# Attention and expert-layer kernel: layer norm of the first attention's scores by centred context and mean square, head rebuilt, routing of the second half of the tokens moved into the shared unit

## What is computed

```python
x = x + attention1(layernorm(x), ctx)      # kv = ctx @ W.T + b ; out = p @ kv ; sim = out @ kv.T / 16
                                           # softmax(layernorm(sim) * gamma + beta)
x = x + experts(layernorm(x))              # 8 experts, top 2, capacity 160 each for first and second choice, plus a shared one
x = x + attention2(ctx, ctx, layernorm(x)) # softmax(q.k * layernorm(x), masked)
x = x + lut_ffn(layernorm(x))              # silu(gate) * up, down; weights looked up in a table of 16
```

## Time and profile before

| | us |
|---|---|
| median of 3 runs | 328.35 |
| lowest, highest | 326.55, 332.02 |
| the profiled execution, its own time | 328.0 |
| its span in the trace | 326.3 |
| mean granted clock of PE, share of full speed | 0.965 |

### The profile page before, as it was taken

How to read it: one execution, slowest core, us unless ns; L and a number is a source line. 1 busy time by engine, 2 the same in 40 slices (tenths; PEclk the granted TensorE clock), 3 DMA queues, 4 the chain that set the end, 5 groups by cost and what they waited for, 6 DMA issues and landing times.

```text
span 326.3 us, 6015 instructions
## 1 busy us (share of the span) xinstructions
PE 305.4 (94%) x1944; PEld 262.5 (80%) x1944; DVE 239.2 (73%) x650; ACT 151.3 (46%) x358; POOL 111.6 (34%) x153
## 2 busy tenths in 40 slices
PE   8998567997999999999999999999999989979995
PEld 4654355776989899898989999899888879879994
DVE  3658987413499989898998989898986749866632
ACT  2466437533346455564546555565633532541210
POOL 7473644770000605032150604123062226234331
PEclk9998769999899999999999999999999999979998
DMA  7994018335167664939375574828033000010101
GB/s 230 371 265 105 7 42 268 123 113 148 48 178 249 142 220 97 308 63 294 94 212 167 129 252 72 294 52 229 3 40 131 1 0 2 0 35 0 34 1 64
DMA packets 26259, 41.48 MB, mean 127 GB/s; under 512 B 3898, under 2 KB 16955, under 8 KB 26236
## 3 DMA queue, kind: packets, MB, share of 16 engines
q1 hardware_dynamic: 22012, 36.46, 35.2%
q0 software_dynamic: 4224, 4.75, 8.2%
HBM read 31.37 MB, written 9.82 MB: 126 GB/s over the span
## 4 chain that ended last, share of the span: by engine, by line
PE 78%; DVE 9%; POOL 4%; issue 3%; ACT 3%; DMA 1%; SPq 0%; POOLq 0%
PE hb L715 25%; PE yb L734 24%; PE hb L849 10%; PE yb L748 5%; PE tb L648 3%; PE rb L864 3%; PE yb L553 2%; POOL xbuf_dram L498 2%; PE yb L864 1%; DVE x L1249 1%; DVE bst L1104 1%; DVE xn L1110 1%; DVE xT_lo L1262 1%; POOL rstd L461 1%; DMA xbuf_dram<-xn,put_i 1%
## 5 line engine op out<-in xcount | busy, mean ns | idle before, releaser
L734 PE MATMUL yb<-raw,h 128*128 128x256 f32 x384 | 96.7, 382 | 0.0
L1015 ACT ACTIVATE h<-hb,b 128x320 f32<-128x320 f32 (+1 forms) x80 | 44.6, 559 | 70.1 <-PE hb L715 68.7
L734 PEld LDWEIGHTS yb<-raw,h 128*128 128x128 f32 x384 | 70.3, 192 | 7.5 <-ACT h L1015 0.4
L715 PE MATMUL hb<-xT_hi,w_hi 128*128 128x320 f32 (+1 forms) x180 | 72.6, 403 | 1.4 <-DVE xT_lo L1262 1.4
L518 POOL DMA_INDIRECT xacc_dram<-ysb,slot_i x16 | 25.5, 1594 | 126.1 <-ACT ysb L883 123.6
L715 PE MATMUL hb<-xT_lo,w_hi 128*128 128x320 f32 (+1 forms) x180 | 59.3, 329 | 0.0
L715 PE MATMUL hb<-xT_hi,w_lo 128*128 128x320 f32 (+1 forms) x180 | 59.2, 329 | 0.0
L1454 DVE TENSOR_TENSOR w_lo<-raw,w_hi 128x256 fp32r<-128x256 f32 x81 | 33.6, 415 | 22.3 <-ACT w_hi L883 22.2
L1136 DVE COPY_PREDICATED pick<-bits,pick 128x536 int32<-128x536 uint8 x56 | 42.7, 762 | 0.6
L715 PEld LDWEIGHTS hb<-xT_hi,w_hi 128*128 128x128 f32 x180 | 34.4, 191 | 6.6 <-issue 2.0
L715 PEld LDWEIGHTS hb<-xT_hi,w_lo 128*128 128x128 f32 x180 | 34.6, 192 | 2.5
(11 more groups left out here) (205 smaller groups left out, 523.4 us busy)
## 6 DMA issues: line engine op xcount, KB each, us to landing
raw<-w1pack_dram SPq DMA_DIRECT2D x30, 384.0 KB, 3.5
raw<-w2pack_dram SPq DMA_DIRECT2D x30, 384.0 KB, 5.5
xbuf_dram<-h SPq DMA_DIRECT2D x8, 323.8 KB, 10.0
idx<-idx_dram SPq DMA_DIRECT2D x8, 268.0 KB, 6.1
xg<-xbuf_dram SPq DMA_DIRECT2D x8, 259.0 KB, 5.9
x<-x_dram SPq DMA_DIRECT2D x4, 256.0 KB, 4.4
xacc_dram<-x SPq DMA_DIRECT2D x2, 512.0 KB, 7.0
x<-xacc_dram SPq DMA_DIRECT2D x4, 256.0 KB, 4.6
```

The source lines that it names most:

```text
L715: mm = pe.matmul(hb[s % RING][:, 0:n], w[:, s, k * P:(k + 1) * P], a[:, turn, k, 0:n], start=(i == 0), stop=(i == len(terms) - 1))
L734: mm = pe.matmul(yb[c // 2][:, (c % 2) * D:(c % 2 + 1) * D], h, w, start=(s == 0 and c % 2 == 0), stop=(s == STEPS - 1), skip_group_check= ...
L1015: act.activation(hidden(s - 1, shared, turn), bank[:, 0:n], ACT.Gelu, bias=b1[:, expert, s - 1:s])\
```

## The change

1. **Centred context.** DVE sums each batch of `ctxT` over its 256 columns and forms `ctxc` = 256*ctx - sum (`centre`). `kvT` is projected from it without the bias row (`project`), so the scores come out with mean zero, times 256. 
2. **Mean square.** ACT squares the scores out of PSUM with a sum along the row (`squares`); POOL makes 1/sqrt from the sums (`inv_sim`). `sim_stats`, `offsets`, `standard_sim` and `gain` are gone. DVE multiplies the scores in PSUM by 1/std and gamma into SBUF in one instruction per tile, in front of the old row maximum.
3. **Head.** POOL's constants are reordered, with the first two `inv_std` among them. `values` works on half the context at a time. Idle matmuls: 12 in place of 22 ahead of `token_rows(0)`, and their wait for `gate_ok` is now for an instruction that DVE does behind `norm_x` of batches 0 and 1. The last batch's `sim_rows` comes behind `norm_x(2, 1)`; `exps(0, 3)` behind `rows_hi(1)`.
4. **Routing.** On DVE `up_rows(0)` and `low_rows(0)`, which need unit 0's step 0, come ahead of `add_probs(0, 3)`, the normalising of half 1 and `choose(0)`. On PE `token_rows(1)` goes from behind `first(0)` to behind `first(3)`, `count(0)` from there to behind `second(0)`; `logits_of(1)`, `logits_rows(1)`, `count(1)` follow in steps 3 to 5; scores 2 and 3 go from steps 4 and 5 to 6 and 7. ACT does `rows_hi(2)`, `logits_exp(0)` and `logits_copy(1)` behind the Gelu of step 3, `logits_exp(1)` behind that of step 5.

```diff
@@ gpsimd
-            for b in range(B):
-                inv_std(1, b, S * 1e-6)
-                split_lo(b, b)
-                gain(b)
+            inv_sim(0)
+            split_lo(0, 0)
+            inv_sim(1)
+            split_lo(1, 1)
+            inv_sim(2)
+            split_lo(2, 2)
             inv_std(2, 0, 1e-5)
+            inv_sim(3)
+            split_lo(3, 3)
@@ tensor
             pe.wait_ge(gate_ok, 2)
-            pe.wait_ge(proj_sb, 2 + B)
+            pe.wait_ge(consts_ok, CONSTS)
+            pe.wait_ge(kv_sb, 2)
             pe.wait_ge(exp_ok, 4)
-            keep_busy(16, rb)
+            keep_busy(8, rb)
             pe.wait_ge(xn_ok, 2)
-            keep_busy(6, rb)
+            keep_busy(4, rb)
             token_rows(0)
...
                     first(g, u, s, shared, turn)
+                    if u_is(u, 0):
+                        if s == 3:
+                            token_rows(1)
+                        elif s == 4:
+                            logits_rows(1)
+                        elif s == 5:
+                            count(1)
...
                         second(u, 0, shared, turn, loads)
+                        if u_is(u, 0):
+                            count(0)
@@ scalar
+            def squares(b):
+                act.wait_ge(sim_mm, b + 1)
                 for i in range(2):
                     tile = 2 * b + i
-                    act.activation(exp_rows(0, b)[:, i, :], hb[b % RING][:, i * S:(i + 1) * S], ACT.Identity,
-                                   bias=nmr[:, tile:tile + 1], scale=rstd[:, 1, tile:tile + 1]).then_inc(sm_in, 1)
+                    act.activation(exp_rows(0, b)[:, i, :], hb[b % RING][:, i * S:(i + 1) * S], ACT.Square,
+                                   accum_out=ssq[:, tile:tile + 1]).then_inc(ssq_ok, 1)
...
+            exps(0, 0)
+            squares(2)
+            outT_copy(3)
+            split_hi(0, 0, 0)
+            squares(3)
+            exps(0, 1)
...
-                        if s == 1:
+                        if s == 3:
+                            rows_hi(2, 1, UTOK)
+                            logits_exp(0)
                             logits_copy(1)
-                        elif s == 2:
+                        elif s == 5:
                             logits_exp(1)
@@ vector
+            def centre(b):
+                cols = slice(b * S, (b + 1) * S)
+                if b == 0:
+                    dve.wait_ge(ctx_in, 32)
+                own(dve.tensor_reduce(ctx_sum[:, b:b + 1], ctxT[0:H, cols], AX.X, ALU.add))
+                dve.tensor_scalar(ctxc[:, cols], ctxT[0:H, cols], float(S), ctx_sum[:, b:b + 1], ALU.mult, ALU.subtract)\
+                    .then_inc(ctxc_ok, 1)
...
+                    dve.scalar_tensor_tensor(out=exp_rows(0, b)[:, i, :], in0=hb[b % RING][:, i * S:(i + 1) * S],
+                                             scalar=rstd[:, 1, tile:tile + 1], in1=gamma[:, :],
+                                             op0=ALU.mult, op1=ALU.mult).then_inc(sm_in, 1)
...
             norm_x(2, 0, xn_ok)
+            norm_x(2, 1, xn_ok)
+            dve.wait_ge(gate_ok, 1)
+            dve.tensor_tensor(gate_parts[:, :, E:2 * E], gate_w[:, :, :], gate_parts[:, :, 0:E].bitcast(F32),
+                              ALU.subtract).then_inc(gate_ok, 1)
             sim_rows(3)
...
-            choose(0)
-            route(0)
-            rows_lo(2, 1, UTOK)
...
+            add_probs(0, 2, 2)
             up_rows(0, 0)
+            low_rows(0, UTOK)
+            add_probs(0, 3, 2)
+            norm_x(2, 2, xn_ok)
+            norm_x(2, 3, xn_ok)
+            choose(0)
+            rows_lo(2, 1, UTOK)
+            route(0)
             unit(0, 0, shared=True, extra=unit0_extra)
```

More of the change, by code:

```diff
@@ L468, in split_lo @@
                     .then_inc(w_lo_ok, 1)
[L470 to L483 removed]
+            inv_std(0, 2, 1e-5)
+            inv_std(0, 3, 1e-5)
+            inv_sim(0)
[4 more added lines that the diff above has]
+            split_lo(2, 2)
             inv_std(2, 0, 1e-5)
+            inv_sim(3)
+            split_lo(3, 3)
             inv_std(2, 1, 1e-5)
[L486 to L487 removed]
+            split_lo(4, 4)
+            split_lo(5, 5)
             inv_std(2, 2, 1e-5)
@@ L557, in _, with values, project @@
             pe.wait_ge(ctx_in, 32)
-            for n in range(2):
-                pe.matmul(hb[n][0:H, :], projw[:, 0, :], ctxT[:, n * 512:(n + 1) * 512], start=True, stop=True)\
-                    .then_inc(proj_mm, 1)
-            pe.wait_ge(consts_ok, CONSTS)
+            def values(half):
+                for j in range(HT * half, HT * half + HT):
+                    mm = pe.matmul((hb[2], rb)[half][:, j * H:(j + 1) * H],
+                                   ctxT[:, j * P:(j + 1) * P], projw[:, 0, :], start=True, stop=True)
+                mm.then_inc(kv_mm, 1)
+            def project(n):
+                pe.wait_ge(ctxc_ok, 2 * n + 2)
+                pe.matmul(hb[n][0:H, :], projw[0:H, 0, :], ctxc[:, n * 512:(n + 1) * 512], start=True, stop=True)\
+                    .then_inc(kvT_mm, 1)
             def transpose_p(b):
+                if b == 0:
+                    pe.wait_ge(ident_ok, 1)
                 pe.wait_ge(p_ok, 2 * b + 2)
@@ L593, in similar @@
                 mm.then_inc(sim_mm, 1)
-            def values(b):
-                for j in (2 * b, 2 * b + 1):
-                    mm = pe.matmul(hb[2][:, j * H:(j + 1) * H] if b == 0 else rb[:, j * H:(j + 1) * H],
-                                   ctxT[:, j * P:(j + 1) * P], projw[:, 0, :], start=True, stop=True)
-                mm.then_inc(proj_mm, 1)
-            keep_busy(12, yb[1])
+            values(0)
+            keep_busy(7, yb[1])
+            project(0)
+            keep_busy(2, yb[1])
             transpose_p(0)
-            values(0)
-            transpose_p(1)
+            values(1)
             keep_busy(3, yb[1])
             mix(0)
-            values(1)
+            transpose_p(1)
             keep_busy(2, yb[1])
             similar(0)
+            keep_busy(2, yb[1])
             mix(1)
+            project(1)
             transpose_p(2)
-            values(2)
             keep_busy(3, yb[0])
@@ L617, in _ @@
             transpose_p(3)
-            values(3)
             keep_busy(3, yb[1])
@@ L987, in _ @@
             score_copy(1)
+            rows_hi(1, 0, UTOK)
             exps(0, 3)
-            rows_hi(1, 0, UTOK)
             logits_copy(0)
@@ L992, in _ @@
                 split_hi(j, j, 0)
-            logits_exp(0)
-            rows_hi(2, 1, UTOK)
             act.wait_ge(bias_in, 16)
@@ L1396, in unit @@
                 for s in range(STEPS):
-                    if s == 1:
+                    if s == 1 and u:
                         low_rows(u, UTOK if shared else SLOTS)
```

181 lines of the change are left out of this document (80 added, 101 removed).

## The result

| | before | after |
|---|---|---|
| median, us | 328.35 | 339.52 (5 runs, 337.07 to 339.65) |
| the profiled execution, its own time | 328.0 | 337.07 |
| its span | 326.3 | 335.3 |
| first scatter starts | 53.07 | 62.95 |
| PE's transposes of expert 1 | 78.69 | 88.60 |

The ratio is 1.0371, 95% interval 1.0335 to 1.0407: slower, as forecast.

A forecast was written before the change was run, and what follows sets the result against it. Units bound by PE, head by DVE; the 25.6 us chain from first scatter to expert 1's transposes had 0.20 us of slack. First scatter 10.1 late: 328.0 + 10.0 = 338.0 us, range 331.5 to 341.5.

The forecast's parts named there:

- `norm_x(2, 1)` ends: Head, DVE: the normalising of batch 1 ends at 35.9, 3.5 us sooner than the 39.37 before.
- unit 0 begins: PE: unit 0 starts at 44.4, 0.9 sooner, with 5.9 unchanged from `token_rows(0)` to `first(0)`.
- PE's wait for the load: Unit 0's end: PE idles 7 to 11 us ahead of the `xg` transposes, until expert 1's rows are loaded.
- The multiplication of the scores in PSUM with gamma: Head, DVE: four new multiplications, 0.34 to 0.45 each, 1.5 us together (1.3 to 2.0).
- POOL's queue held batch 1: Head: batch 1's 1/sqrt stands behind weight block 0's split on POOL, so DVE starts its rows at about 24.1.
- the idle matmuls behind `gate_ok`: Head, PE: 12 idle matmuls wait for DVE behind the normalisations and run before `token_rows(0)`, 2.4 us.
- rival 1: Head: POOL's splits miss DVE and PE's clock is up (gate logits -0.9); scatter 5 us late, 333; chance 0.19.
- From `token_rows(1)` to the first scatter: Unit 0's routing: transposes, `second(0)`, Gelu, copies, table load, exponential and `route` in a row, 8.3 us.
- From the first scatter to the transposes: 16 scatters in a row, landing and load of expert 1's rows: 25.6 us, not shortened by the change.
- half 1's slots would not be late next: Routing: eight scatters take 10.2 us, PE has 7.7 between the counts, so half 1's slot numbers are in time.
- The third rival: ACT: a table switch costs more than its load, exponential ahead of `route` up to 1.3 later: 339.3; chance 0.04.
- the prediction's upper end: Range top 341.5, including 1.2 if expert 1's transposes and the stage behind them run at the low clock.

The follow-up runs named there:

- The table of two by two: First scatter's start in profiled executions: old head, old routing 53.07; old head, new routing 63.31; new head, old routing 54.53; new head, new routing 62.95.
- the last version: Changed kernel with part 4 undone, `gate_parts` earlier on DVE and 36 small ACT copies ahead of `rows_hi(1)`: median 330.32, ratio 0.998 to the kernel before.
- the last version without the copies: Changed kernel with part 4 undone and `gate_parts` earlier on DVE, no 36 small ACT copies: 329.38 and three executions at 334.7 to 334.9.

## Why the prediction was right

It said 338.0, and the median is 339.52, inside the range. Its steps, in the order of the chain:

| step | said | measured |
|---|---|---|
| DVE starts on batch 1's rows | 24.1 | 24.29 |
| `norm_x(2, 1)` ends | 35.9 | 36.40 |
| `token_rows(0)` | 38.5 | 39.07 |
| unit 0 begins | 44.4 | 43.77 |
| `lowrank` ends | 49.7 | 49.13 |
| `token_rows(1)` | 54.9 | 54.38 |
| first scatter | 63.2 | 62.95 |
| last scatter | 82.8 | 82.36 |
| PE done with unit 0 | 79 | 80.1 |
| PE's wait for the load | 7 to 11 | 8.53 |
| transposes of expert 1 | 88.8 | 88.60 |
| time of the profiled execution | 338.0 | 337.07 |

The mechanism is shown: in the changed kernel's trace PE waits 8.53 for a load that stands as far behind the first scatter as before, delaying the first scatter alone costs nearly its delay, halving the scatters takes the loss away, and part 4 alone puts the first scatter back. Some of the closeness is luck. `token_rows(0)` came 0.6 later than said and unit 0 began 0.6 sooner, two errors of opposite sign; and the 0.9 behind the transposes, which brings the profiled execution from 338.0 to 337.07, has a cause that the forecast did not have.

**The head.** The multiplication of the scores in PSUM with gamma, which no row of before showed, took 0.44 for each (two in 0.88), the upper end of the 0.34 to 0.45 given. POOL's queue held batch 1 as said. What DVE won there did not reach PE for the reason given, the idle matmuls behind `gate_ok` (2.74, said 2.4); moving that wait gave 2.5 us at `token_rows(0)`. Two sizes were off. Unit 0 began 4.7 behind `token_rows(0)`, not 5.9: the transposes took 1.58 where they had taken 1.97, and from the first gate-logit matmul to unit 0 it took 1.11 and not 1.88. PE's granted clock was 0.90 from 42 to 44, where it was 0.50 before. So this part of rival 1's condition came true and gave 0.8 of the 0.9 that it was priced at; the rest of the rival did not come true. And the 0.9 by which the prediction had unit 0 begin sooner is not what the head is worth for the scatters. The table of two by two shows it 1.5 late with the old routing, because of the add that moved; the prediction did not take this apart, as `lowrank` covered it.

**The routing.** From `token_rows(1)` to the first scatter it took 8.57, said 8.3. From the first scatter to the transposes 25.65, said 25.6. That half 1's slots would not be late next was right for this kernel: its `put_i` came at 69.66, 7.9 behind half 0's, and its turn to scatter was at 73.42. It is not so everywhere. In four kernels with the old routing, the first scatter between 52.59 and 56.71, POOL stood 1.8 to 3.3 ahead of the ninth scatter (68.18, 64.97, 69.15 and 66.16), each time behind a DVE that had stood for 4.3 to 5.8.

**The tables.** The third rival had the exponential over 1 us behind its load. It started 0.01 behind it, at 60.28, and 0.02 behind the second one. The Trainium skill (ScalarE: Activation LUTs, What ACT_TABLE_LOAD costs) has about 1.38 us of drain with each switch; the measurement decides, and no drain shows on this path.

**What is off.** The sum was made against the profiled execution and gave 338.0 where that took 337.07. The 0.9 is behind the transposes (246.7 against 247.6), and the traces say where. Up to the third of the four groups of transposes in the table-lookup feed-forward (289.66 before, 299.86 after) the changed kernel takes 0.3 more; its transposes of `xg` and the matmuls behind them ran at a granted clock of 0.50 (88.6 to 94), as the prediction's upper end allowed. The fourth group then comes 13.6 behind the third (313.48) and not 15.1 (304.78), since in the kernel before PE ran at 0.51 from 289.6 to 293.0, and in the changed one at 1.00 over the same work. Of these 1.5, 0.3 are lost again up to the end. Both stretches stand behind an idle time of 2.1 (2.06 and 2.08), so what decides the clock there is not shown. The median lies 2.45 above the profiled execution; the four timed executions have no trace here. The kernel before has such a spread as well, and stalls and slow starts of the two kinds below are of the right size. That they are the cause is not shown.

## What to carry to other kernels

Find the strand that leaves one engine's timeline and comes back: here a chain of one-at-a-time scatters and a load, which showed no wait only because it started early enough. Its slack (0.2 us) is the most that anything ahead of its first instruction may slip, and smoothing the waits of the busy engine in front of that point is worth nothing. In a queue that is worked off in order, one instruction that waits for a later stage (`low_rows` for unit 0's Gelu) taxes everything behind it. And where a kernel has several such chains, a single profile of one execution does not tell its median; look at the list of times for groups first.

## What the runs showed that I had not expected

**Engines stand still, in some executions, while POOL's indirect DMAs run.** In unit 0, ACT, and for shorter times DVE, stood with their inputs there. The longest gaps on ACT were 9.00 (up to 77.67, last scatter at 74.51), 11.80 (up to 86.28, last at 82.72), 13.24 (81.98, 78.41), 11.26 (80.56, 80.66) and 8.42 (76.31, 77.29, in the kernel whose scatters were delayed); in the last version ACT and DVE went on at the same moment, 64.15 and 64.07. The changed kernel's own profiled execution has none, with all sixteen scatters, and the new head with the old routing has executions at 329.77 and at 339.5, of which only one of the slower has a trace. I suspect that the engines' own program is fetched late behind the scatters, but the one test of this, moving ACT's place in its program, did not decide it. The Trainium skill (Runtime: NRT & Kernel Launch, Instruction fetch mechanics) calls the cost of passing from one block of program to the next mostly hidden. No run here shows whether this standstill is that cost.

**PE at half its usual speed in the head, at a granted clock recorded as full.** In the profiled execution of the last version without the copies (334.78) PE's matmuls up to about 17 take nearly twice as long. PE's timeline, first that execution, then the one of the kernel with the copies:

```profile
11.74 1.80 PE L580 MATMUL rb<-projw,ctxT 65*128 65x64 f32 x8
```

```profile
9.29 1.00 PE L581 MATMUL rb<-projw,ctxT 65*128 65x64 f32 x8
```

The granted clock reads 1.00 over 5 to 20 in both. The durations are near those of the low level: seven idle matmuls took 0.23 each in the first (6.95 to 8.58) and 0.12 each in the second (6.76 to 7.62), and in the changed kernel twelve took 0.21 each where the clock reads 0.50 (36.53 to 39.07). So the record of the clock may be wrong there; no run decides it. The scores of the second attention began 5.0 later (34.35 against 29.34), the transposes of expert 1 were 3.0 later (84.21 against 81.22), and the whole execution took 2.8 more (334.78 against 331.95). What decides it in a given execution stays open.
